# Probabilities of an attention loop transposed through memory instead of on TensorE, for all four units of a period

## The chip, the cores and the metric

One core of one Trainium2 chip runs the whole program. The metric is the device time of one execution in microseconds. Its engines are TensorE (PE, matrix products; PEld is its weight load), VectorE (DVE), ScalarE (ACT), GpSimd (POOL) and SyncE (SP, which here only issues transfers); 16 DMA engines carry the transfers of all queues.

## What is computed

A cross attention and then a routed feed-forward layer, each added to its input. The attention has 16 sequences (b), 256 queries and 256 keys each, 16 heads of 64:

```python
q = (x @ w_q).reshape(B, Sq, HEADS, DIM_HEAD).transpose(0, 2, 1, 3)
k = (context @ w_k).reshape(B, Skv, HEADS, DIM_HEAD).transpose(0, 2, 1, 3)
v = (context @ w_v).reshape(B, Skv, HEADS, DIM_HEAD).transpose(0, 2, 1, 3)
sim = jnp.einsum('bhid,bhjd->bhij', q, k) * SCALE
attn = jax.nn.softmax(sim, axis=-1)
out = jnp.einsum('bhij,bhjd->bhid', attn, v)
...
x = x + _L0_xattn_ref(_layernorm(x, axis=-1), ctx_768, ...)
x = x + _L0_ffn_ref(_layernorm(x, axis=-1), ...)
```

The feed-forward layer scores each of 4096 rows for 8 experts, takes the best two, sends rows to experts with room for 640 each, and sums the two experts' outputs by their gates. All numbers are float32; products that need it are made of three terms, a high part and a rest of each operand (`qh`, `ql` and so on).

## The kernel before

**Periods.** The attention loop has 64 periods, m = 0 to 63, four to a sequence: b = m // 4, r = m % 4. A period has four units, one head each. Its stages are `scores` (L801, into PSUM banks 0 to 3), row maxima `max0` to `max3` on DVE (L1255), exponentials `exp0` to `exp3` on ACT (L1067, into `prob`), and two periods later `pv` (L839), which multiplies transposed probabilities `probt` with `v`. In between the probabilities are transposed. `q`, `k` and `v` are the projections for the next period (L734); their halves are written by ACT (`q_hi`, `k_hi`) and DVE (`q_lo`, `k_lo`). The result of `pv` is multiplied by the inverse sums in place in PSUM (`a_norm`, L1274), and split into `ah` (ACT, `a_hi`) and `al` (DVE, `a_lo`). `o` (L855) is the output projection, twice a sequence, `xt` and `x2t` are transposes of a sequence's rows, `logits` and `pos` belong to the routing, as do `bias`, `shift`, `compare`, `rank`, `gate`, `slot`, `keys` and `pick` on DVE and `scatter` on POOL (L668), which writes rows into the experts' table in memory.

**Two ways to transpose.** In the moved periods (`MOVED`, 6 to 61) units 0 and 1 go through memory: DVE transposes 32x32 squares in place (`square0`, `square1`, L1279), SP writes the half to memory (`lift`, L485) and, once it has landed, reads it back with four transfers that put the squares in their places (`move`, L492). Units 2 and 3 are transposed on PE (`turn2`, `turn3`, L819, four transposes against the identity each) and copied out of PSUM by ACT (`copy2`, `copy3`, L1007). In the other periods all four units are turned on PE.

**Inverse sums.** DVE takes them (`inv`), SP writes them out (`inv_out`, L466) and reads them back spread over partitions (`inv_in`, L475), into one buffer `invrows`; so `inv_in` of period m - 1 waits for the `a_norm` of period m - 2.

**Order.** `timeline()` writes down one list of stages; each engine runs its own stages of that list in that order. Waits are on semaphores. Products other than scores and turns share three PSUM banks in turn (`WORKS`, `bank`); each waits until the user of its bank three before has been read. `logits` and the turns use bank 4.

**After the loop** come the expert products, in the stretch from about 700 us on, which nothing here touches.

## Time and profile before

| | us |
|---|---|
| median of three runs | 956.02 |
| lowest and highest | 954.73, 957.37 |
| the profiled execution | 957.82 |
| its span, first to last instruction | 956.1 |

| engine | busy us | share |
|---|---|---|
| PE | 918.1 | 96% |
| DVE | 739.8 | 77% |
| ACT | 573.8 | 60% |
| POOL | 280.2 | 29% |

The page of the profile gives such shares for the whole span. Views of a stretch give them for that stretch; the chain of waits gives, from start to start, what each piece took on the way to the end. A line such as L819 is a line of the kernel above; L734, L1007 and L1201 are helpers that several stages share.

### The profile page before, as it was taken

How to read it: one execution, taken by the hardware profiler on the slowest of the kernel's cores; microseconds unless marked ns; L12 is line 12 of the kernel's file. 1: busy time of each engine (PE TensorE's matmuls, PEld its weight loads, DVE VectorE, ACT ScalarE, POOL GpSimd, SP SyncE). 2: the span in 40 equal slices, each digit the busy share in tenths (PEclk: the TensorE clock that was granted, in tenths of full speed). 3: DMA queues.
4: the chain of work that ended last, by engine and by line, in shares of the span. 5: the costliest groups of instructions: out<-in, count | busy, mean ns of one | idle time of the engine just before them, and what ended most of it. 6: DMA issues, size and time to landing. Idle time of an engine off the chain costs nothing.

```text
span 956.1 us, 22462 instructions
## 1 busy us (share of the span) xinstructions
PE 918.1 (96%) x7916; PEld 821.0 (86%) x7916; DVE 739.8 (77%) x1745; ACT 573.8 (60%) x1600; POOL 280.2 (29%) x441
## 2 busy tenths in 40 slices
PE   7999999999999999999999999999889999999995
PEld 7878888888888888888888888888689999999995
DVE  5757778888888888888888888877777877678762
ACT  5877766667667666766766677676534433334420
POOL 5541112314233231323223132302533223322233
PEclk9999999999999999999999999999899999999999
DMA  8462535445455445455444445444345765645422
GB/s 239 143 205 91 163 123 163 162 152 168 146 157 158 148 157 164 136 172 164 139 156 161 146 130 170 136 134 136 121 133 99 149 145 123 135 84 98 112 29 27
DMA packets 152991, 133.29 MB, mean 139 GB/s; under 512 B 62140, under 2 KB 141610, under 8 KB 152752
## 3 DMA queue, kind: packets, MB, share of 16 engines
q1 hardware_dynamic: 144048, 122.87, 42.9%
q0 software_dynamic: 8832, 8.98, 5.4%
q8 instruction: 64, 1.05, 0.5%
q14 instruction: 47, 0.39, 0.1%
HBM read 82.15 MB, written 54.61 MB: 143 GB/s over the span
## 4 chain that ended last, share of the span: by engine, by line
PE 70%; DVE 11%; ACT 10%; issue 4%; DMA 3%; POOL 0%; SPq 0%; POOLq 0%; ACTq 0%; DVEq 0%
PE psum L734 20%; PE psum L839 9%; PE psum L996 9%; PE psum L855 9%; PE psum L980 8%; PE psum L801 7%; ACT prob L1067 6%; PE psum L819 5%; DVE negmax L1255 3%; DVE hidl L1201 2%; DVE bufl L1201 1%; ACT probt L1007 1%; DVE hidh L1488 1%; PE psum L879 1%; DVE psum L1274 1%
## 5 line engine op out<-in xcount | busy, mean ns | idle before, releaser
L1067 ACT ACTIVATE prob<-psum,negmax 128x256 f32<-128x256 f32 x512 | 238.0, 481 | 79.5 <-DVE negmax L1255 79.4
L1255 DVE TENSOR_REDUCE negmax<-psum 128x2 f32<-128x512 f32 x256 | 160.4, 682 | 29.7 <-PE psum L801 29.7
L1173 ACT ACTIVATE hid<-psum,b1t 128x640 f32<-128x640 f32 x64 | 50.9, 795 | 126.6 <-PE psum L980 125.0
L839 PE MATMUL psum<-probt,v 128*64 128x256 f32 x1024 | 124.6, 385 | 0.0
L707 POOL DMA_INDIRECT out_rows<-y,rowi x40 | 66.3, 1658 | 160.8 <-DVE y L1498 154.2
L1067 ACT ACTIVATION_READ_ACCUMULATOR prob<-psum,negmax 128x1 f32 x512 | 109.5, 214 | 0.0
L839 PEld LDWEIGHTS psum<-probt,v 128*64 128x64 f32 x1024 | 67.8, 136 | 36.4 <-issue 0.3
L668 POOL DMA_INDIRECT slot_table<-row,picki x64 | 66.8, 1044 | 96.9 <-PE psum L734 61.2
L996 PE MATMUL psum<-w2h,hidh 128*128 128x256 f32 x320 | 91.4, 286 | 2.9 <-DVE y L1498 1.5
L801 PE MATMUL psum<-kh,qh 64*128 64x256 f32 x512 | 82.5, 316 | 11.1 <-ACT prob L1067 8.9
L996 PE MATMUL psum<-w2l,hidh 128*128 128x256 f32 x320 | 90.5, 283 | 0.0
L996 PE MATMUL psum<-w2h,hidl 128*128 128x256 f32 x320 | 90.5, 283 | 0.0
L1007 ACT ACTIVATE probt<-psum 128x512 f32<-128x512 f32 x144 | 87.3, 609 | 4.4 <-PE psum L819 4.4
L819 PE MATMUL psum<-ident,prob 128*128 128x128 f32 x576 | 87.1, 276 | 2.7 <-ACT prob L1067 2.7
L734 PE MATMUL psum<-xth,wqh 128*128 128x256 f32 x256 | 78.9, 308 | 0.5 <-DVE xtl L1201 0.5
L1279 DVE STREAM_TRANSPOSE prob<-prob 128x512 f32<-128x512 f32 x112 | 78.6, 702 | 0.0
L855 PE MATMUL psum<-woh,ah 128*128 128x256 f32 x256 | 72.9, 285 | 1.6 <-DVE al L1201 1.6
L606 POOL TENSOR_SCALAR shifted<-ln_mean_var 128x2 f32<-128x2 f32 x32 | 7.1, 223 | 225.0 <-issue 182.7
L801 PE MATMUL psum<-kl,qh 64*128 64x256 f32 x512 | 72.9, 278 | 0.0
L801 PEld LDWEIGHTS psum<-kh,qh 64*128 64x128 f32 x512 | 48.8, 185 | 27.9 <-ACT prob L1067 13.3
L801 PE MATMUL psum<-kh,ql 64*128 64x256 f32 x512 | 72.8, 277 | 0.0
L855 PE MATMUL psum<-wol,ah 128*128 128x256 f32 x256 | 72.4, 283 | 0.0
(199 smaller groups left out, 2704.6 us busy)
## 6 DMA issues: line engine op xcount, KB each, us to landing
squares<-prob SPq DMA_DIRECT2D x56, 512.0 KB
probt<-squares SPq DMA_DIRECT2D x224, 128.0 KB, 2.8
invrows<-inverses SPq DMA_DIRECT2D x128, 128.0 KB
w1r<-in_w SPq DMA_DIRECT2D x8, 1024.0 KB
w2r<-in_w SPq DMA_DIRECT2D x8, 1024.0 KB, 9.1
slot_table<-blank SPq DMA_DIRECT2D x8, 662.5 KB, 6.5
blocks<-slot_table SPq DMA_DIRECT2D x56, 80.0 KB
xin<-in_x SPq DMA_DIRECT2D x16, 256.0 KB, 3.5
```

Source lines behind the costliest of these rows:

```text
L668: pool.indirect_dma_start(out=table, out_offset=bass.IndirectOffsetOnAxis(ap=picki[:, b % 3, k, t:t + 1], axis=0), in_=row[:, b % 3, t, :] ...
L734: mm = pe.matmul(dst, lhs, rhs, start=(j == 0), stop=(j == len(terms) - 1))
L801: mm = pe.matmul(psum[:, 2 * cc + h, qb * S:(qb + 1) * S], a[r, m % 2, cc, cols], w[r, m % 2, cc, :], start=(j == 0), stop=(j == len(terms ...
L819: mm = pe.transpose(psum[:, TURN_BANK[u], kb * S + qb * P:kb * S + (qb + 1) * P], prob[:, m % 2, u, kb, qb, :], ident[:, :])
L839: mm = pe.matmul(dst[h * HD:(h + 1) * HD, cc * S:(cc + 1) * S], v[:, b % 2, kb, cols], p, start=(kb == 0), stop=(kb == ST - 1))
L855: mm = pe.matmul(dst[:, 0:D], a[:, b % 2, c, tt], w[:, c, :], start=(c == 0 and j == 0), stop=(c == PAIRS - 1 and j == 2))
L980: mm = pe.matmul(dst, lhs, rhs, start=(n == 0), stop=(n == len(terms) - 1))
L996: mm = pe.matmul(dst, a[:, j, ss], w[:, j, :], start=(j == 0 and m == 0), stop=(j == HC - 1 and m == 2))
L1007: copy = lambda dst, src, **kw: act.activation(dst, src, ACT.Copy, **kw)
L1067: last = act.activation(into, out_of, ACT.Exp, bias=negmax[:, m % 2, u, qb:qb + 1], accum_out=total[:, m % 2, u, qb:qb + 1])
L1255: dve.tensor_reduce(negmax[:, m % 2, u, :], psum[:, u, :].rearrange("p (q s) -> p q s", q=ST), AX.X, ALU.max, negate=True).then_inc(sem("m ...
L1279: dve.transpose(at, at).then_inc(sem("square"), 1)
```

## The change

All four units of a moved period go through memory. `by_pe` is empty there, so PE has no `turn2` and `turn3` and ACT no copies. DVE transposes two units in one instruction, twice a period. `lift` writes 1 MB instead of 512 KB, and the four reads take 256 KB each in rows of 2 KB; SP issues two of them (`move_low`) and ACT the other two, behind its last exponential of the next period (`move_high`). An exponential now waits for the lift of two periods before, not for the moves.

`invrows` has two buffers, so `inv_in` waits for the `a_norm` of a period earlier, and `a_norm` stands behind `k_lo`. It writes to a new buffer `attended` in SBUF instead of PSUM, and the bank is free once it is done. A fourth work bank comes in with bank 4, and `logits` takes a work bank. Three pieces of DVE work go to POOL: `a_lo` (periods 4 to 59), `ln1` of later sequences, and the second half of `pick` (DVE keeps its two reductions as `extremes`). `x2t` moves from r = 2 to r = 3, `logits` and `bias` to r = 0, where `shift`, `compare`, `rank` and `gate` stand in both. The context has one load buffer instead of two. The core of the diff:

```diff
+POOL_REST = range(PER_B, PERIODS - 4)
...
-    return (2, 3) if m in MOVED else (0, 1, 2, 3)
+    return () if m in MOVED else (0, 1, 2, 3)
...
-        out += [("scores", m)] + ([("pv", m - 2)] if m >= 2 else [])
-        out += [("logits", b - 2)] if r == 3 and 2 <= b else []
...
         else:
-            out += [("q", m + 1), ("turn2", m - 1), ("k", m + 1), ("turn3", m - 1), ("v", m)]
+            out += [("scores", m)] + ([("logits", b - 3)] if r == 0 and 3 <= b else [])
+            out += [("q", m + 1), ("k", m + 1), ("pv", m - 2), ("v", m)]
...
         else:
-            out += [("copy2", m - 1), ("k_hi", m + 1), ("exp2", m), ("copy3", m - 1), ("exp3", m), ("v_sb", m)]
+            out += [*steps("exp0 exp1", m), ("q_hi", m + 1), ("exp2", m), ("k_hi", m + 1), ("exp3", m),
+                    ("move_high", m - 1), ("a_hi", m - 2), ("v_sb", m)]
...
-        out += ([("a_norm", m - 2)] if m >= 2 else []) + [("inv", m - 1)]
...
-        out += ([("a_lo", m - 2)] if m >= 2 else []) + [("q_lo", m + 1)]
-        out += [("square0", m)] if m in MOVED else []
-        out += [("k_lo", m + 1)]
...
+        else:
+            out += [("inv", m - 1)] + ([("slot", b - 3)] if r == 2 and 3 <= b else [])
+            out += [("x2add", ST * (b - 2) + 1)] if r == 1 and 2 <= b else []
+            out += [("bias", b - 3)] if r == 0 and 3 <= b else []
+            out += [("q_lo", m + 1), ("square0", m), ("k_lo", m + 1), ("a_norm", m - 2)]
...
-            out += [("ln1", b + 1)] if 1 <= b < B - 1 else []
...
-        out += [("pick", b - 3)] if r == 3 and 3 <= b else []
...
+        out += [("ln1", b + 1)] if r == 0 and 1 <= b < B - 1 else []
         out += [("scatter", b - 4)] if r == 0 and 4 <= b else []
         out += [("residual", b + 1)] if r == 0 and 1 <= b < B - 1 else []
+        out += [("a_lo", m - 2)] if m - 2 in POOL_REST else []
...
-        out += steps("inv_out inv_in", m - 1) + (steps("lift move", m) if m in MOVED else [])
+        out += [("extremes", b - 3), ("pick", b - 3)] if r == 3 and 3 <= b else []
...
+        out += [("inv_out", m - 1)] + ([("move_low", m - 1)] if m - 1 in MOVED else [])
+        out += [("traffic", b - 2)] if r == 1 and 2 <= b else []
+        out += [("inv_in", m - 1)] + ([("lift", m)] if m in MOVED else [])
...
-WORK_READ = {"xt": "xt_lo", "q": "q_lo", "k": "k_lo", "v": "v_sb", "pv": "a_lo", "o": "x2", "x2t": "x2t_sb",
+WORK_READ = {"xt": "xt_lo", "q": "q_lo", "k": "k_lo", "v": "v_sb", "pv": "a_norm", "o": "x2", "x2t": "x2t_sb",
...
+def places():
...
+    banks, last, found = [5, 6, 7], {}, {}
+    for stage, n in TIMELINE:
+        work = stage.removesuffix("_most"), n
+        if (stage, n) == ("turn0", PERIODS - 2):
+            banks.remove(4)
+            found[stage, n] = 4, last[4]
+        if work in WORKS and work not in found:
+            at = banks.pop(0)
+            banks.append(at)
+            found[work] = at, last.get(at)
+            last[at] = work
+        if (stage, n) == ("turn3", MOVED[0] - 1):
+            banks.append(4)
+    return found
+
...
-        invrows = sb(rest, "invrows", [2, S])
+        invrows = sb(rest, "invrows", [2, 2, S])
...
+        def move(eng, m, groups):
+
+            eng.wait_ge(sem("lifted"), 16 * (m - MOVED[0] + 1))
+            eng.wait_ge(sem("pv"), m - 1)
+            for g in groups:
+                eng.dma_start(probt_all(m)[g * SQ:(g + 1) * SQ, :].rearrange("j (a c) -> j a c", a=GROUPS),
+                              square_table[m % 2].rearrange("(a j) (g c) -> g j a c", a=GROUPS, g=GROUPS)[g])\
+                   .then_inc(sem(f"moved{m % 2}"), 16)
+
...
-                if m >= 1:
-                    sp.wait_ge(sem("a_norm"), m)
+                if m >= 2:
+                    sp.wait_ge(sem("a_norm"), m - 1)
                 for h in range(2):
-                    sp.dma_start(invrows[h * HD:(h + 1) * HD, :, :],
+                    sp.dma_start(invrows[h * HD:(h + 1) * HD, m % 2, :, :],
                                  inv_table[m % 2][0:UNITS * ST].rearrange("(c h q) p -> h c (q p)", h=2, q=ST)[h]
                                  .partition_broadcast(HD))\
...
-                sp.dma_start(square_table[m % 2], prob_pair(m)).then_inc(sem("lifted"), 16)
...
+                sp.dma_start(square_table[m % 2], prob_all(m)).then_inc(sem("lifted"), 16)
...
+            def ln1(b):
+                pool.wait_ge(sem("xt"), b)
+                if b >= XRING:
+                    pool.wait_ge(sem("logits"), b - XRING + 1)
+                for t in range(ST):
+                    last = pool.tensor_scalar(xn[:, t, :], xin[:, b % XRING, t, :], mean_var["ln1"][:, t, 0:1],
+                                              rstd["ln1"][:, t:t + 1], ALU.subtract, ALU.mult)
+                last.then_inc(sem("ln1"), 1)
...
+            def a_lo(m):
+                b, c = divmod(2 * m, PAIRS)
+                pool.wait_ge(sem("a_hi"), m + 1)
...
+                pool.tensor_tensor(al[:, b % 2, c:c + 2, :], attended[:, :, :],
+                                   ah[:, b % 2, c:c + 2, :].bitcast(F32), ALU.subtract).then_inc(sem("a_lo"), 1)
+
+            def pick_(b):
+                pool.wait_ge(sem("extremes"), b + 1)
+                if b >= 3:
+                    pool.wait_ge(sem(f"scatter{b % 3}"), 16 * 2 * ST * (b // 3))
+                pool.tensor_scalar(pick[:, 0, :], pick[:, 0, :], BIG, None, ALU.add)
+                link(pool.tensor_scalar(pick[:, 1, :], pick[:, 1, :], -1.0, None, ALU.add))
+
+                link(pool.tensor_tensor(same[:, 0, :], pick[:, 1, :], pick[:, 0, :], ALU.subtract))
+                link(pool.tensor_scalar(same[:, 0, :], same[:, 0, :], 0.0, BIG, ALU.is_le, ALU.mult))
+                link(pool.tensor_tensor(pick[:, 1, :], pick[:, 1, :], same[:, 0, :], ALU.add))
+                pool.tensor_copy(picki[:, b % 3, :, :], pick[:, :, :]).then_inc(sem("picks"), 1)
...
-                    pool.wait_ge(sem("q"), PER_B * (b + 4) + 2)
+                    pool.wait_ge(sem("k"), PER_B * (b + 4) + 2)
...
-                            if m in MOVED and cc == 0:
-                                p = probt_pair(m).rearrange("p (a u k q i) -> p u k q a i", a=GROUPS, u=2, k=ST, q=ST)[:, h, kb]
+                            if m in MOVED:
+                                p = probt_all(m).rearrange("p (a u k q i) -> p u k q a i", a=GROUPS, u=UNITS, k=ST,
+                                                           q=ST)[:, 2 * cc + h, kb]
                             else:
                                 p = probt[:, m % 2, 2 * cc + h, kb, :]
...
+                if m >= 2 and m - 2 not in MOVED:
                     act.wait_ge(sem("turn"), turns_to(m - 2, u))
                 elif m >= 2:
-                    act.wait_ge(sem(f"moved{m % 2}"), 16 * moves_to(m - 2))
+                    act.wait_ge(sem("lifted"), 16 * (m - 2 - MOVED[0] + 1))
                 for qb in range(ST):
...
-                dve.wait_ge(sem("inv_in"), 32 * (m + 1))
-                at = work_bank("pv", m).rearrange("p (c s) -> p c s", c=2)
-                dve.tensor_tensor(at, at, invrows[:, :, :], ALU.mult).then_inc(sem("a_norm"), 1)
-
-            def square(m, u):
-                dve.wait_ge(sem("exp"), UNITS * m + u + 1)
-                at = prob_pair(m).rearrange("p (g u c) -> p u g c", g=GROUPS, u=2)[:, u]
+                dve.wait_ge(sem(f"inv_in{m % 2}"), 32 * (m // 2 + 1))
+                if m >= 1:
+                    dve.wait_ge(sem("a_lo"), m)
+                dve.tensor_tensor(attended[:, :, :], work_bank("pv", m).rearrange("p (c s) -> p c s", c=2),
+                                  invrows[:, m % 2, :, :], ALU.mult).then_inc(sem("a_norm"), 1)
+
+            def square(m, pair):
+
+                dve.wait_ge(sem("exp"), UNITS * m + 2 * pair + 2)
+                at = prob_all(m).rearrange("p (g v c) -> p v g c", g=GROUPS, v=2)[:, pair]
                 dve.transpose(at, at).then_inc(sem("square"), 1)
...
+            def extremes(b):
+                dve.wait_ge(sem("keys"), b + 1)
+                if b >= 1:
+                    dve.wait_ge(sem("picks"), b)
+                dve.tensor_reduce(pick[:, 0, :], lowkey[:, :, :], AX.X, ALU.min)
+                dve.tensor_reduce(pick[:, 1, :], high_of(b), AX.X, ALU.max).then_inc(sem("extremes"), 1)
```

The order of the instructions shows it at three places. On PE, in a moved period, `q` is followed by the turn of a unit and then `k` before:

```order
L734 MATMUL psum<-xth,wql 128x256
L819 MATMUL psum<-ident,prob 128x128 [waits s_exp]
L819 MATMUL psum<-ident,prob 128x128 x3
L734 MATMUL psum<-c0h,wkh 128x256 [waits s_ctx,s_v_sb]
L734 MATMUL psum<-c0l,wkh 128x256
L734 MATMUL psum<-c0h,wkl 128x256
```

and after, where `k` ends and `pv` and `v` follow:

```order
L797 MATMUL psum<-c1s,wkh 128x256
L797 MATMUL psum<-c1s,wkl 128x256
L904 MATMUL psum<-probt,v 64x256 [waits s_probt,s_moved1,s_v_sb]
L904 MATMUL psum<-probt,v 64x256 x7
L797 MATMUL psum<-wvh,c0h 128x512 [waits s_ctx,s_x2]
```

No turn stands there, and `pv` has moved from ahead of `q` to behind `k`. On DVE, in a period with r = 3 (`negmax` are the maxima, `invrows` the inverse sums, `prob` the squares, `pick` and `picki` the routing's slots), before:

```order
L1255 TENSOR_REDUCE negmax<-psum 128x2 [waits s_scores] x4
L1274 TENSOR_TENSOR psum<-psum,invrows 128x512 [waits s_inv_in,s_pv]
L1264 RECIPROCAL invtot<-total 128x8 [waits s_inv_out,s_exp]
L1267 STREAM_TRANSPOSE invturned<-invtot 128x32 [waits s_inv_total]
L1334 TENSOR_TENSOR logit<-psum,rb_all 128x16 [waits s_logits]
L1201 TENSOR_TENSOR al<-psum,ah 128x512 [waits s_a_hi]
L1244 SCALAR_TENSOR_TENSOR ql<-psum,qh 128x512 [waits s_q_hi]
L1279 STREAM_TRANSPOSE prob<-prob 128x4x128 [waits s_exp]
L1201 TENSOR_TENSOR kl<-psum,kh 128x512 [waits s_k_hi]
L1279 STREAM_TRANSPOSE prob<-prob 128x4x128 [waits s_exp]
L1431 TENSOR_REDUCE pick<-lowkey 128x2 [waits s_scatter1,s_keys]
L1432 TENSOR_REDUCE pick<-highkey 128x2
```

and after:

```order
L1325 TENSOR_REDUCE negmax<-psum 128x2 [waits s_scores] x4
L1334 RECIPROCAL invtot<-total 128x8 [waits s_inv_out,s_exp]
L1337 STREAM_TRANSPOSE invturned<-invtot 128x32 [waits s_inv_total]
L1314 SCALAR_TENSOR_TENSOR ql<-psum,qh 128x512 [waits s_q_hi]
L1352 STREAM_TRANSPOSE prob<-prob 128x4x256 [waits s_exp]
L1271 TENSOR_TENSOR kl<-psum,kh 128x512 [waits s_k_hi]
L1345 TENSOR_TENSOR attended<-psum,invrows 128x512 [waits s_a_lo,s_inv_in1,s_pv]
L1352 STREAM_TRANSPOSE prob<-prob 128x4x256 [waits s_exp]
L1502 TENSOR_REDUCE pick<-lowkey 128x2 [waits s_picks,s_keys]
L1503 TENSOR_REDUCE pick<-highkey 128x2
```

`al` is gone, the squares are twice as long, and the multiplication by `invrows` stands behind `kl` and waits for POOL's `a_lo` of the period before. On ACT the end of a period with r = 0 is after:

```order
L1072 ACTIVATE kh<-psum 128x512 [waits s_scores,s_k]
L1133 ACTIVATE prob,total<-psum,negmax 128x2x4x32 [waits s_lifted,s_max]
L1133 ACTIVATE prob,total<-psum,negmax 128x2x4x32
L433 DMA probt<-squares 32x4x512 [waits s_pv,s_lifted]
L433 DMA probt<-squares 32x4x512
L1072 ACTIVATE ah<-attended 128x512 [waits s_o,s_a_norm]
L1072 ACTIVATE v<-psum 128x512 [waits s_pv,s_v]
L1191 ACTIVATE lexp<-lshift 128x16 [waits s_shifted]
```

The two copies into `probt` are gone, two transfers stand behind the last exponential, and `ah` has moved behind them. On POOL a period with r = 0 now holds the context, `ln1`, the four scatters, the residual and then `a_lo`; before it held the context, the scatters and the residual. Its scatters wait for `k` now and waited for `q`.

## Rows read from the trace of the kernel before

**Rows 1.** The page, busy us (share of the span) and instructions of each engine.

```profile
PE 918.1 (96%) x7916; PEld 821.0 (86%) x7916; DVE 739.8 (77%) x1745; ACT 573.8 (60%) x1600; POOL 280.2 (29%) x441
```

**Rows 2.** Busy time by stretch, one sequence; last: granted clock, DMA share, GB/s.

```profile
390.57:432.61 42.04, 41.30 (x380) 35.58 (x379) 35.34 (x93) 29.11 (x92) 11.68 (x23) 1.00 0.49 157
```

**Rows 3.** The chain of waits, 417 to 442: start us, us, engine, tile, line.

```profile
420.57 0.42 PE psum L879 x16
...
430.10 1.64 PE psum L734 x12
431.74 0.44 PE psum L819 x4
432.18 1.19 PE psum L734 x10
...
433.80 1.16 PE psum L734 x5
434.96 2.86 PE psum L855 x24
437.82 1.62 PE psum L801 x24
439.44 1.88 PE psum L839 x16
```

**Rows 4.** PE's timeline: start, duration, instruction, [idle before, who ended it].

```profile
410.71 0.39 PE L734 MATMUL psum<-c0h,wkh 128*128 128x256 f32 x1 [0.26 <-DVE valid L1382]
...
427.25 0.39 PE L801 MATMUL psum<-kh,qh 64*128 64x256 f32 x2 [0.49 <-ACT prob L1067]
```

**Rows 5.** The chain of waits again, a `pv` ahead of the moved periods.

```profile
71.20 1.88 PE psum L839 x16
```

**Rows 6.** DVE's transposes, whole span: count, busy us, mean ns of one.

```profile
L1279 DVE STREAM_TRANSPOSE prob<-prob 128x512 f32<-128x512 f32 x112 | 78.6, 702 | 0.0
...
L1470 DVE STREAM_TRANSPOSE turned<-blocks 128x640 f32<-128x640 f32 x14 | 11.6, 834 | 0.0
```

**Rows 7.** DVE's timeline in a period with r = 3.

```profile
424.92 0.69 DVE L1201 TENSOR_TENSOR kl<-psum,kh 128x512 fp32r<-128x512 f32 x1 [0.33 <-ACT kh L1007]
425.53 0.70 DVE L1279 STREAM_TRANSPOSE prob<-prob 128x512 f32<-128x512 f32 x1
...
426.39 0.17 DVE L1433 TENSOR_SCALAR pick<-pick 128x2 f32<-128x2 f32 x1
...
427.30 2.47 DVE L1255 TENSOR_REDUCE negmax<-psum 128x2 f32<-128x512 f32 x4
```

**Rows 8.** Busy time by stretch of 1 us, during a lift and during moves.

```profile
407.00:408.00 1.00, 1.00 (x13) 0.64 (x10) 1.00 (x3) 0.20 (x1) 0.54 (x3) 1.00 0.90 359
411.00:412.00 1.00, 1.00 (x10) 1.00 (x10) 1.00 (x2) 0.78 (x2) 0.00 (x0) 1.00 0.82 266
```

**Rows 9.** SP's waits (total us, times, longest), and its timeline: one period's moves.

```profile
SPq L492 <- DMA squares<-prob: 174.1, 56, 4.8
...
421.35 1.75 SPq L492 DMA_DIRECT2D probt<-squares  x4
```

**Rows 10.** POOL in one sequence, and in its timeline behind the scatters.

```profile
L631 POOL TENSOR_TENSOR xin<-xin,bo_all 128x256 f32<-128x256 f32 x2 | 1.5, 727 | 2.2 <-DMA slot_table<-row,picki 2.1
...
440.59 1.54 POOL L631 TENSOR_TENSOR xin<-xin,bo_all 128x256 f32<-128x256 f32 x2 [2.95 <-DMA slot_table<-row,picki]
```

**Rows 11.** DVE's groups in one sequence: idle before them, who ended it.

```profile
L1255 DVE TENSOR_REDUCE negmax<-psum 128x2 f32<-128x512 f32 x16 | 10.0, 681 | 1.2 <-PE psum L801 1.2
...
L1244 DVE SCALAR_TENSOR_TENSOR ql<-psum,qh 128x512 fp32r<-128x512 f32 x5 | 3.4, 690 | 1.1 <-ACT qh L1007 1.0
...
L1201 DVE TENSOR_TENSOR kl<-psum,kh 128x512 fp32r<-128x512 f32 x4 | 2.8, 692 | 1.0 <-ACT kh L1007 0.6 <-issue 0.3
...
L1201 DVE TENSOR_TENSOR xtl<-psum,xth 128x512 fp32r<-128x512 f32 x1 | 0.7, 691 | 1.1 <-ACT xth L1007 1.1
```

**Rows 12.** Busy time by stretch, the opening.

```profile
0.00:24.00 24.00, 18.70 (x148) 17.04 (x149) 13.86 (x23) 13.62 (x34) 12.73 (x26) 1.00 0.86 239
```

More of the change, by code:

```diff
@@ L214 @@
 TIMELINE = timeline()
-WORK_BANKS = 3
 TURN_BANK = (4, 0, 1, 4)
-APART = {**{("logits", b): 4 for b in range(B - 3)}, ("x2t", B - 2): 2, ("logits", B - 2): 3, ("pos", B - 2): 4, ("logits", B - 1): 4}
+APART = {("x2t", B - 2): 2, ("logits", B - 2): 3, ("pos", B - 2): 4, ("logits", B - 1): 4}
 GATHER = ((2, 3), (0, 1))
@@ L685, in _ @@
                     inverse_root(stage[:3], n)
+                if stage == "ln1" and n >= 2:
+                    ln1(n)
+                if stage == "a_lo" and n in POOL_REST:
+                    a_lo(n)
+                if stage == "pick" and n < B - 4:
+                    pick_(n)
                 if stage == "vsplit":
@@ L714, in _ @@
         def _(pe):
-            work = {w: n for n, w in enumerate(WORKS)}
             def bank(stage, n):
-                if stage == "logits" and n < B - 3:
-                    pe.wait_ge(sem("probt"), turns_to(PER_B * (n + 2) + 1, UNITS - 1))
-                    return psum[:, APART[stage, n], :]
                 if (stage, n) in APART:
@@ L1453, in _ @@
             for stage, n in TIMELINE:
-                if stage in steps:
+                if stage in steps and not (stage == "ln1" and n >= 2 or stage == "a_lo" and n in POOL_REST
+                                               or stage == "pick" and n < B - 4):
                     steps[stage](n)
```

139 lines of the change are left out of this document (72 added, 67 removed).

## The prediction, made before the changed kernel was run

> **What bounds the kernel now.** I read the page's busy shares first [rows 1]: TensorE (PE) is busy 918.1 of 956.1 us, VectorE (DVE) 739.8, ScalarE (ACT) 573.8, GpSimd (POOL) 280.2. PE is the bound, but an average does not say where the changed part stands, so the second view cuts the attention loop into rounds. A round is one sequence, four periods. A round takes 42.04 us (three in a row differ by 0.01), and in it PE is busy 41.3, DVE 35.35, ACT 29.1 and POOL 11.7 us at granted clock 1.00; the DMA engines have a share of 0.49 at 157 GB/s [rows 2]. Third comes the chain of waits, since its pieces show what each stage costs PE from start to start, without the overlap that the busy numbers count [rows 3]: scores 1.62, pv 1.88, q 1.64, k 1.19, v 1.16, o 2.86, logits 0.42, and each turn, four transposes, 0.44 us. xt and x2t are four transposes as well; pos, five tiny products, I put at 0.2.
>
> The round adds up. Without turns it is 4 x (1.62 + 1.88 + 1.64 + 1.19 + 1.16) = 29.96, plus 2 x 2.86, plus 0.44 + 0.44 + 0.42 + 0.2: **37.2 us of PE work**. The eight turns are 8 x 0.44 = 3.5. The remaining 42.04 - 37.2 - 3.5 = 1.3 us are gaps, and two of them can be seen: k waits 0.26 us for `valid`, that is for a bank, and scores wait 0.49 us for an exponential [rows 4].
>
> **The change, part by part.** *Turns removed.* In the 56 moved periods (14 rounds) PE loses turn2 and turn3: 112 x 0.44 = 49.3 us. PE does nothing in their place. The moved operand is read by pv in runs of 32 elements, for two units before and four after; that costs nothing, since pv took 1.88 us at 71.20, before any period was moved, and takes 1.88 us in the moved rounds [rows 3, 5]. ACT, busy 29.1 of 42 us, loses eight copies a round and gains eight DMA issues, about as much again; it stays far from a bound.
>
> *Double squares on DVE.* 128x512 takes 702 ns and 128x640 834 ns [rows 6]: 1.03 ns an element, so 128x1024 should take 1.23 us, 0.53 more than now. That is 8 x 0.53 = +4.2 us a round. Taken off DVE: four `al`, which step like `kl` by 0.61 us (424.92 to 425.53; -2.4), ln1's two applications (half an `al` each, -0.6), and five of the seven picking instructions (426.39 to 427.30, -0.9) [rows 7]. Net +0.3: DVE has some **35.7 us of work a round against PE's 37.2**. This is what makes the change close.
>
> *The order inside a period.* I lay a period out from the start of its scores, with the pieces above. PE: q done at 3.3, k at 4.5, pv at 6.3, v at 7.5. DVE: maxima from 0.95 to 3.4, inverse to 3.8, q_lo from 4.15, square0 to 5.9, k_lo to 6.5, a_norm (behind pv) to 7.1, square1 to 8.25, then the period's extras. ACT: exp3 ends near 6.3. Periods are 10.8 (r=0), 8.1 (r=1), 10.4 (r=2) and 7.9 us (r=3) of PE work; DVE's extras are 2.6, 2.0, 3.0 and 0.2 us. So DVE begins the maxima up to 0.9 us late behind r=1 and 0.7 late behind r=2, and is level again in r=3, whose extras are the smallest. The next scores need exp3 and k_lo, which are ready at 6.3 to 7.4 us even then, ahead of the shortest period's end at 7.9. PE does not wait on this path, with 0.5 to 3 us to spare. Both visible gaps should go: the exponentials no longer stand behind copies, and the fourth work bank gives `valid` a turn more.
>
> *Transfers.* Each lift is 1 MB and each period moves 1 MB. A round now carries 157 GB/s x 42 us = 6.6 MB [rows 2]; with 2.1 MB more each way it carries 10.8 MB. Engine time: 0.49 x 42.04 = 20.6 us now. A stretch with little but a lift ran at 359 GB/s with a share of 0.90, 401 at a full share; one with moves and other small packets at 266 GB/s with 0.82, 324 at a full share [rows 8]. The moves' packets double to 2 KB, so they lie between. Adding 2.1 MB at 401 and 2.1 MB at 324 to 401 gives 31.0 to 32.3 us in a round of 38: **a DMA share of 0.83**, against 0.49. In time: lifts land 3.1 us behind their issue now (174.1 us for 56) [rows 9]; doubled, about 4.5 to 5. Moves go out once the lift has landed, from SP near 5 us into the next period and from ACT behind exp3 at 6.3 to 7.2 (four issues take 1.75 us now [rows 9]), and land near 11. The pv that reads them starts at 12.5 in the short periods: 1 to 1.5 us to spare, least in r=1, where SP's x, output and context transfers (0.77 MB) run between the two halves.
>
> That the second half is issued from ACT saves SP's issue time only, as far as rows show: one pool of 16 engines carries all queues, and its share is what I sum. The Trainium skill, "DMA: Bandwidth & Descriptors", section "Issuing engines are not separate DMA queues", says the same in general: DMAs started from several engines run on the same 16 DMA engines and interleave, and only the sequencer's issue time is saved. By that rule the second queue brings no bandwidth, which speaks against this part of the change and for the DMA rivals below; by a rule of its own bandwidth for each queue those rivals would have no chance and the forecast would be the same.
>
> *Double inverse rows.* inv_in no longer waits for the a_norm of the same period, so a_norm can stand behind k. Same bytes, cost nothing; the cover is a whole period.
>
> *POOL* gains a_lo, ln1 and the rest of picking. 128x256 takes 727 ns [rows 10], so a_lo takes at most 1.45 us and I take 1.3, a fixed part being paid once; four of them, two ln1 and six small ones add 8 us to 11.7 us. The tight place is r=0: context, ln1, the scatters behind k (4.9 to 10.0), their landing (2.95 us now [rows 10]), residual 1.5, then a_lo done near 15.8. The next a_norm waits for it and could start at 17.1: 1.3 us to spare. If that is lost, DVE stands still with square1 behind it.
>
> *Before and after the moved rounds* the work is the same. At the end SP reaches the expert weights behind two moves instead of four: nothing to 1.5 us gained, I take nothing.
>
> **The sum.** PE's work of 37.2 us is the floor of a round, 42.04 the ceiling of "nothing gained". Of the 1.3 us of gaps I keep 0.9, as room for new waits where DVE and the transfers have about 1 us to spare: a round of 38.1 us. Saved: 3.94 x 14 = 55 us. The profiled execution is 957.8 us, 1.8 over the median 956.0: 957.8 - 55 = 902.6, and 901 against the median.
>
> **Rivals.**
> 1. *All gaps go*: 37.2 us a round, 4.84 x 14 = 68 saved: 888. For it: the laid-out period has no PE wait. Against it: DVE at 96% and DMA at 0.83 of their time.
> 2. *DVE becomes the bound.* If DVE keeps the waits that it has for q_hi, k_hi, xt_hi and the scores (1.0 + 0.6 + 1.1 + 1.2 = 3.9 us [rows 11]), its round is 35.7 + 3.9 = 39.6: 34 saved, 922. For it: they are waits for ACT's results, which the new order also has. Against it: several arise only because PE was behind.
> 3. *Moves land late.* The margin of 1 to 1.5 us in r=1 and r=3 goes, and pv waits 1 us in two periods: a round of 40.1, 27 saved, 929.
> 4. *DMA engines saturate* (slower). The only long stretch with a share near 1 is the opening, 239 GB/s at 0.86 [rows 12]. If squares, moves, broadcasts and scatters together reach only 239 GB/s, a round of 10.8 MB takes 45.2 us: +3.1 x 14 = 44 us, 1000. It decides from 257 GB/s (10.8 MB in 42.04 us) down.
> 5. *The turns go, but their time is idled*, by a chain of lift, move and pv that keeps today's period: 956.
>
> **How the numbers follow.** Forecast 0.50 (37.7 to 39.0 us a round: 895 to 914), rival 1 0.14, rivals 2 and 3 0.23 together, rival 4 0.07, rival 5 0.03, and 0.03 for a round between 40.1 and 42. The range leaves out rivals 4 and 5 and the last, and goes 3 us below rival 1 for the floor's own error: 885 to 935. A measurement of this kernel tells 0.3% (about 3 us) from no change; faster 0.89, same 0.04, slower 0.07.
>
> **What would show it.** Right: a round of about 38 us, PE busy over 95% of it (no transposes of `prob` on PE from the seventh period to the sixty-second), DVE's `prob` transposes near 1.23 us, a DMA share near 0.83. Rival 2 shows as PE idle before scores or before q, k, v, released by DVE, with DVE above 95% busy; rival 3 as PE idle before pv, released by `probt<-squares`; rival 4 as the same with shares near 1 and landings far over 5 us; a late a_lo as DVE idle before `attended`, released by POOL. The forecast is wrong if a round takes over 39.5 us, most likely because margins of 1 us, each laid out from one trace, do not hold together.

## The result and the profile after

The changed kernel takes **985.93 us** (median of 4 runs, 984.21 to 987.17) against 955.75 us (954.73 to 957.37) for the kernel before on the same chip: a ratio of 1.031, 95% interval 1.029 to 1.034. It is slower by 30 us where 55 us were forecast to be saved. The forecast of 901 us, its range (885 to 935) and its sign were wrong.

The page first, as [rows 1]: busy us and shares of each engine.

```profile
PE 891.5 (90%) x7468; PEld 794.0 (81%) x7468; DVE 744.6 (76%) x1601; ACT 510.7 (52%) x1488; POOL 400.8 (41%) x597
```

PE lost 448 instructions, the transposes, and its share fell from 96 to 90%: no engine has become the bound. Next the stretches, one of the loop in the kernel before and one in the changed kernel (columns as in [rows 2]).

```profile
252.00:294.00 42.00, 41.25 (x379) 35.58 (x377) 35.42 (x93) 29.08 (x93) 11.68 (x23) 1.00 0.48 153
```

```profile
252.00:294.00 42.00, 37.43 (x329) 31.79 (x328) 33.11 (x79) 23.76 (x80) 20.27 (x35) 0.96 0.84 252
```

In 42 us PE now does 329 matmuls, where 379 were done with the turns among them. DVE, ACT and POOL are all below 80%, and the DMA share has risen to 0.84. The granted clock is 0.96, between the 2.4 GHz level, at which it stood before, and 1.2 GHz; PE kept stopping in this stretch. The residual addition on POOL, once a round, opens at 238.72, 283.14, 327.66, 372.74 and 416.94 us, and five rounds on at 638.43: **a round takes 44.4 us** on average over these nine, against 42.04 before. The expert part behind the loop did not change (240 us from its first `hid` activation to the end, 241 before). What holds the round is told by the share of the chain of waits (page, part 4, by engine) and the waits for DMA (out, in, total us, times, longest).

```profile
DMA 33%; PE 23%; DVE 15%; SPq 8%; POOL 8%; issue 6%; ACT 6%; POOLq 0%; ACTq 0%; DVEq 0%
```

```profile
SPq L433 <- DMA squares<-prob: 204.9, 55, 6.6
...
POOL xin L692 <- DMA slot_table<-row,picki: 71.5, 11, 7.1
ACT ah L1072 <- DMA squares<-prob: 60.9, 20, 5.0
...
PE psum L904 <- DMA probt<-squares: 39.6, 37, 3.0
```

SP waits 3.7 us for nearly every lift, where it was 3.1 by [rows 9]; and there the wait began with the lift's issue, while now SP first issues `inv_out` and waits for its input, so 3.7 us is only the rest of the landing. ACT waits for lifts too, PE waits for moves, and POOL waits up to 7.1 us for the scatters (2.95 in [rows 10], 3.6 at most before). The landing times (page, part 6: count, size, median us from issue to landing) show how far the transfers have slowed each other.

```profile
squares<-prob SPq DMA_DIRECT2D x56, 1024.0 KB, 7.7
probt<-squares SPq DMA_DIRECT2D x112, 256.0 KB, 4.9
probt<-squares ACTq DMA_DIRECT2D x112, 256.0 KB, 5.8
invrows<-inverses SPq DMA_DIRECT2D x128, 128.0 KB, 6.0
```

The last view is the chain of waits through one round (start us, us, what). In this round it never touches PE.

```profile
352.92 8.97 DMA squares<-prob
361.91 0.31 SPq L433
...
362.27 0.43 SPq L433
...
362.80 0.60 SPq L510
...
363.45 0.60 SPq L510
...
364.15 9.45 DMA squares<-prob
373.62 0.31 SPq L433
...
378.96 6.95 DMA squares<-prob
...
388.62 6.53 DMA squares<-prob
...
397.38 8.95 DMA squares<-prob
```

A lift is issued 2.2 us (once 2.7) after the one before it landed. In between, SP issues two moves (L433) and two reads of inverse rows (L510); once a round (373.62 to 378.96) x, output and context are issued as well, 5.3 us. The four lifts of this round take 8.97 + 9.45 + 6.95 + 6.53 = 31.9 us; the other 12.6 of the 44.5 us from 352.92 to 397.38 are issues. **The loop through SP's queue is closed**: a lift's landing releases the moves of its period (1 MB, on two queues) and the inverse rows (256 KB), and then the next lift, which runs beside them. So the 1 MB lift has 1.25 MB beside it, issued shortly before, and 2304 KB in 7.7 us are 306 GB/s.

This is not the chain of every round. From 90 to 165 and from 307 to 430 us it is made of lifts and SP's issues almost alone; from 210 to 290 us it holds no lift, and 18 to 20% of it is the landing of the scatters, with POOL's and DVE's work behind it. Two chains of nearly the same length run through this kernel, and both have a transfer in them that became slower.

### The profile page after: what moved, and what is told of

Same layout as the page of the kernel before. It is cut to its first block, busy times and chain, and to the rows that moved or that the text cites. A ratio compares the mean times of both kernels' runs of the same rounds, so it can differ in the third digit from the quotient of the medians.

```text
span 985.4 us, 21333 instructions
## 1 busy us (share of the span) xinstructions
PE 891.5 (90%) x7468; PEld 794.0 (81%) x7468; DVE 744.6 (76%) x1601; ACT 510.7 (52%) x1488; POOL 400.8 (41%) x597
## 3 DMA queue, kind: packets, MB, share of 16 engines
q10 hardware_dynamic: 16128, 29.37, 10.0%
## 4 chain that ended last, share of the span: by engine, by line
DMA 33%; PE 23%; DVE 15%; SPq 8%; POOL 8%; issue 6%; ACT 6%; POOLq 0%; ACTq 0%; DVEq 0%
DMA squares<-prob 26%; PE psum L1061 9%; PE psum L1045 8%; DMA slot_table<-row,picki 5%; SPq L510 4%; ACT prob L1133 3%; DVE prob L1352 3%; SPq L433 2%; POOL slot_table L729 2%; PE psum L797 2%; POOL al L659 2%; DVE hidl L1271 2%; PE psum L904 1%; DVE bufl L1271 1%; DVE attended L1345 1%
## 5 line engine op out<-in xcount | busy, mean ns | idle before, releaser
L904 PE MATMUL psum<-probt,v 128*64 128x256 f32 x1024 | 129.0, 394 | 39.6 <-DMA probt<-squares 39.6
L659 POOL TENSOR_TENSOR al<-attended,ah 128x512 fp32r<-128x512 f32 x56 | 72.4, 1293 | 227.2 <-ACT ah L1072 226.3
L1352 DVE STREAM_TRANSPOSE prob<-prob 128x1024 f32<-128x1024 f32 x112 | 138.0, 1232 | 0.7 <-ACT prob L1133 0.7
L904 PEld LDWEIGHTS psum<-probt,v 128*64 128x64 f32 x1024 | 77.4, 140 | 72.3 <-issue 47.5
L1072 ACT ACTIVATE ah<-attended 128x512 fp32r<-128x512 f32 x64 | 40.5, 632 | 179.9 <-DVE attended L1345 97.5
L1133 ACT ACTIVATION_READ_ACCUMULATOR prob<-psum,negmax 128x1 f32 x512 | 114.1, 223 | 0.0
L1345 DVE TENSOR_TENSOR attended<-psum,invrows 128x512 f32<-128x512 f32 x64 | 43.8, 684 | 75.1 <-POOL al L659 55.0
L797 PE MATMUL psum<-xth,wql 128*128 128x256 f32 x256 | 75.1, 293 | 0.0
L797 PE MATMUL psum<-xtl,wqh 128*128 128x256 f32 x256 | 74.9, 293 | 0.0
L797 PEld LDWEIGHTS psum<-xth,wqh 128*128 128x128 f32 x256 | 50.8, 198 | 29.3 <-DVE attended L1345 21.9
```

Of the source, the lines that this page charges most:

```text
L659: pool.tensor_tensor(al[:, b % 2, c:c + 2, :], attended[:, :, :], ah[:, b % 2, c:c + 2, :].bitcast(F32), ALU.subtract).then_inc(sem("a_lo" ...
L797: mm = pe.matmul(dst, lhs, rhs, start=(j == 0), stop=(j == len(terms) - 1))
L904: mm = pe.matmul(dst[h * HD:(h + 1) * HD, cc * S:(cc + 1) * S], v[:, b % 2, kb, cols], p, start=(kb == 0), stop=(kb == ST - 1))
L1133: last = act.activation(into, out_of, ACT.Exp, bias=negmax[:, m % 2, u, qb:qb + 1], accum_out=total[:, m % 2, u, qb:qb + 1])
L1352: dve.transpose(at, at).then_inc(sem("square"), 1)
```

## The experiments

Four theories. **A**: transfers, either by their number of bytes or by this loop. **B**: POOL's chain; in r = 1 `attended` stood still for `al`, and `al` was behind the residual, which waited for scatters:

```profile
375.79 0.69 DVE L1345 TENSOR_TENSOR attended<-psum,invrows 128x512 f32<-128x512 f32 x1 [5.55 <-POOL al L659]
```

```profile
372.74 1.55 POOL L692 TENSOR_TENSOR xin<-xin,bo_all 128x256 f32<-128x256 f32 x2 [6.83 <-DMA slot_table<-row,picki]
374.37 1.29 POOL L659 TENSOR_TENSOR al<-attended,ah 128x512 fp32r<-128x512 f32 x1
```

**C**: ACT, which now stands in front of its moves for the lift (60.9 us above). **D**: the new order itself. All edits are on the changed kernel, timed in three rounds beside the kernel before. The code shows the core of each edit; `...` stands for more of the same kind.

**half_bytes.** The lift carries the first 1024 of 2048 columns, each move 256 of 512.

```
-  sp.dma_start(square_table[m % 2], prob_all(m))
+  sp.dma_start(square_table[m % 2][:, 0:1024], prob_all(m)[:, 0:1024])
...
```

> The changed kernel with every lift cut to 512 KB and every move to 128 KB, as they were before; all instructions, their order and all other transfers stay (so half of what pv reads is old: this kernel leaves out half of the transposed probabilities). Theory A, transfers: a lift lands 7.7 us behind its issue because the moves of the period before and the inverse rows run beside it, and SP, which issues the next lift only behind that landing, closes the loop. Then a lift lands in 3.5 to 4.5 us, a round falls from 44.5 to 38 or 39 us, and the time to 895 to 915 us. Theory B, POOL: residual waits for the scatters, al behind it, and DVE's attended for al, 5 us a round. The scatters would still have the same place: 950 to 985. Theory C, ACT stands still at its move behind the lift: as A, since the lift lands earlier. Theory D, DVE's longer squares and the new order themselves: 975 to 986.

Measured 915.46 us, ratio 0.956 (0.953 to 0.957). A round takes 39.6 us, at the upper edge of what A foretold. Of the theories, A is right: 70 of the 85 us between forecast and result hang on 59 MB. D can't be the cause, since the longer squares and the new order are all still there.

**short_loop, residual_first, one_queue.** Three changes of order, bytes untouched. In short_loop SP issues inverse rows and traffic ahead of the moves, so that the next lift follows the moves at once; in residual_first POOL's residual comes ahead of the scatters; in one_queue all four moves are SP's.

```
-  out += [("inv_out", m - 1)] + ([("move_low", m - 1)] if m - 1 in MOVED else [])
+  out += steps("inv_out inv_in", m - 1)
   out += [("traffic", b - 2)] if r == 1 and 2 <= b else []
-  out += [("inv_in", m - 1)] + ([("lift", m)] if m in MOVED else [])
+  out += [("move_low", m - 1)] if m - 1 in MOVED else []
+  out += [("lift", m)] if m in MOVED else []
```

> The changed kernel with SP's order in a period as inv_out, inv_in, traffic, move_low, lift, so that between one lift's landing and the next lift's issue SP has only two issues (0.8 us) instead of 2.2 us and in every fourth period 5.2. Theory A, if the loop through SP is what binds: about 4 x 1.3 + 3 = 8 us less a round, down to the next bound of 38 to 40 us: 905 to 930. Theory A, if the rate of the DMA engines binds (share 0.83 now, all transfers still meet): the landing grows by what the loop loses, 965 to 985. Theories B, C and D: no change, 980 to 990.

> The changed kernel with POOL's residual ahead of the scatters instead of behind them, so that al of that period no longer waits for the scatters to land. Theory B: DVE's wait for al (55.0 us in 11 times) goes, 930 to 950. Theory A: the loop through SP sets the round; the chain of waits runs through it and not through POOL, so 975 to 986. C and D: as A.

> The changed kernel with all four moves issued by SP and none by ACT. Theory C: ACT's 61 to 70 us at the lift's landing go, and what follows from them: 930 to 960. Theory A, loop: two more issues of 0.43 us between landing and next lift, 56 periods, 0.9 us each: 1020 to 1035; theory A, rate: 980 to 1000. B and D: no change.

Measured: short_loop 1047.67 us (ratio 1.094, 1.092 to 1.096), residual_first 989.79 (1.034, 1.031 to 1.036), one_queue 1021.09 (1.066, 1.064 to 1.068). residual_first took `al` out of DVE's waits (55.0 us before the edit, none of note after it) and gained nothing, so B alone is not the bound. From 100 to 600 us its chain of waits now runs over the lifts throughout, 50 to 82% of each 100 us: with the one chain gone, the other sets the same time. one_queue took lifts off ACT's path and lost 35 us; the two issues of some 0.4 us that it adds to the loop in each of 56 periods are worth that and more (48 us), so C falls. short_loop was a miss of its expectation, and its waits say why (SP's own; then PE's):

```profile
SPq L511 <- DMA inverses<-invturned: 184.0, 62, 7.3
```

```profile
PE psum L905 <- DMA probt<-squares: 89.8, 39, 6.0
```

`inv_in` waits for a small write (`inverses`, 16 KB) that now has to pass the same 16 engines as the big ones; SP waited up to 7.3 us for it (2.5 at most before). Put ahead of the moves, this wait holds them back. In the changed kernel SP waited for this write only 8 times, 18.8 us in all, since the moves stood in between.

**act_moves2, split_lift.** Two attempts to open the loop with the bytes kept. In act_moves2 ACT issues all four moves, so that no lift stands behind one; in split_lift the lift is two halves in 1 KB rows, each issued when its square is done.

```
+  for half in range(2):
+      if half:
+          sp.wait_ge(sem("square"), 2 * (m - MOVED[0] + 1))
+      sp.dma_start(square_table[m % 2].rearrange("p (g v c) -> v p g c", g=GROUPS, v=2)[half],
+                   prob_all(m).rearrange("p (g v c) -> p v g c", g=GROUPS, v=2)[:, half])
...
```

> The bytes of the changed kernel, but all four moves are issued by ScalarE and none by SyncE, so that a lift on SyncE no longer stands behind the landing of the lift before it. If the loop through SyncE's queue sets the time: 940 to 965 us. If the rate of the DMA engines sets it: 980 to 990 us. If ScalarE's wait for the lift is what costs, it now stands before four issues instead of two: over 990 us.

> The bytes of the changed kernel, but the lift is two transfers of 512 KB in rows of 1 KB, each issued as soon as its own half of the probabilities is turned (about 4 us between them). If the closed loop from turn to landing to the next lift sets the time, the first half lands before the second starts and the loop shrinks by 2 to 3 us in a period: 945 to 970 us. If the rate of the 16 DMA engines sets it, the bytes are as many: 980 to 990 us.

Measured 1027.33 us (1.073, 1.071 to 1.075) and 999.13 us (1.044, 1.042 to 1.046). Both missed what the loop through SP alone foretells. In act_moves2 SP no longer waits for a lift, but the lifts' median landing rises to 8.8 us and the moves' to 6.1, and PE stands 93.9 us for them (39.6 in the changed kernel). It may be that a lift that leaves earlier meets more of the moves before it. But the edit also closes another loop: all moves now stand behind ACT's exponentials. In its chain of waits the last exponentials of a period end at 324.77 us, ACT issues the moves to 326.33, a move lands 9.88 us later, and `pv` follows. The expectation had this as its third case (over 990 us), and the two were not told apart. split_lift did not open the loop: lifts and SP's issues fill its chain of waits from 300 to 600 us. It has eight times the packets in its lifts (1 KB instead of 8 KB each) and one more issue in the loop; those two were not told apart either. So neither run says whether the queue alone is the cause; the runs with fewer bytes do.

**half_lift, half_moves.** Which half of the added bytes costs? In half_lift the lift carries 512 KB and the moves are whole; in half_moves it is the other way about.

> The lift of a period carries 512 KB instead of 1 MB; the four moves keep their size (each reads one half again, so the probabilities are wrong there). Half of the added bytes go. If the loss is the number of bytes: halfway between half_bytes and the changed kernel, 945 to 955 us. If the loop from turn to lift landing to the next lift sets the time, more than half is won, since the 7.7 us landing is what shrinks: 920 to 935 us.

> The lift is whole (1 MB), and each of the four moves carries 128 KB instead of 256 KB (half of the transposed probabilities is left out). If the loss is the number of bytes: 945 to 955 us, as half_lift. If the loop through the lift's landing sets the time, less is won, since only what runs beside the lift shrinks: 955 to 970 us.

Measured 967.67 us (1.010, 1.008 to 1.013) and **913.99 us** (0.955, 0.953 to 0.957). Both expectations missed. With half the moves the whole loss is gone, though each lift still carries 1 MB. The 18 lifts on its chain of waits took 4.0 to 6.6 us (6.5 to 9.8 in the changed kernel), with half the moves beside them; two of them:

```profile
314.18 4.93 DMA squares<-prob
...
355.60 4.09 DMA squares<-prob
```

and the loop is open most of the time (lifts are 10% of the chain over the span, 26% in the changed kernel). Of SP's waits, in the changed kernel the first row was the lift's; in half_moves:

```profile
SPq L501 <- DVE invturned L1337: 255.9, 63, 9.4
...
SPq L433 <- DMA squares<-prob: 41.0, 28, 3.0
...
SPq L520 <- DVE prob L1352: 24.6, 31, 2.8
```

SP waits mostly for DVE's inverse sums (L1337) and squares (L1352) of the next period, as it should, and 41.0 us for lifts where it was 204.9. In half_lift the lifts, half as large, still landed in 7.2 us beside whole moves. But half_lift had a fault of its own, seen in the queues (page, part 3; packets, MB, share), first of the changed kernel and then of half_lift; q10 carries ACT's moves alone:

```profile
q10 hardware_dynamic: 16128, 29.37, 10.0%
```

```profile
q10 hardware_dynamic: 16128, 29.37, 13.8%
```

0.100 x 16 x 985.4 us over 16128 packets is 98 ns each, 0.138 x 16 x 966.6 is 132. In half_lift moves of two queues read the same bytes at the same time.

**half_lift_b, thin_rows.** half_lift with each move reading its own part; and the changed kernel with the inverse rows cut to 32 of 256 columns.

```
+  few = slice(0, 1024 if m > MOVED[0] + 1 else 2048)
+  sp.dma_start(square_table[m % 2][:, few], prob_all(m)[:, few])
```

> half_lift mended: there two moves on two queues read the same half of the table, and a packet of ScalarE's moves took 132 ns against 98 ns in the changed kernel. Here the lift carries 512 KB from the third middle period on, and each move reads its own part of the table, partly stale. If that double reading was what set half_lift (967.7 us) apart from half_moves (914.0 us): 915 to 925 us. If full moves are what the program can't take, whoever lifts: 955 to 970 us.

> The changed kernel, with the two inverse-row reads of each middle period cut to 32 of 256 columns (32 KB in place of 256 KB; the other rows are stale there). They are issued between the moves and the next lift and run beside both. If the time is that of the bytes in flight (2.25 MB in 7.7 us, so 0.75 us for 224 KB), each of 56 periods gets shorter by that: 986 - 42 = 944, so 935 to 955 us. If the small packets of these reads cost nothing beside the large ones: 980 to 986 us.

Measured 939.12 us (0.980, 0.977 to 0.982) and 954.79 us (0.995, 0.991 to 0.999). half_lift_b lies between its two expectations. Reading the same bytes twice had cost half_lift 29 us; a packet of ACT's moves now takes 107 ns. thin_rows gains 31 us for 224 KB a period, 0.55 us of every period where 0.75 was expected. By bytes alone (70 us for 59 MB) these 12.6 MB would have been worth 15. The round follows what is in flight together: with 2304, 2080 and 1792 KB (changed kernel, thin_rows, half_lift_b) it takes 44.4, 42.6 and 41.2 us. But half_moves, also 1792 KB, takes 39.3, so the number of bytes is not all. That whole moves cost more than whole lifts is shown; in half_lift_b they land in 4.7 to 5.7 us and PE still stands 11.7 us before `pv`, in half_moves in 2.9 to 3.1 and it doesn't. The queues say where the time goes (as above; half_moves, then half_lift_b):

```profile
q1 hardware_dynamic: 127920, 137.55, 47.4%
q10 hardware_dynamic: 16128, 14.69, 5.6%
```

```profile
q1 hardware_dynamic: 127920, 123.92, 48.9%
q10 hardware_dynamic: 16128, 29.37, 11.5%
```

With almost the same bytes the two queues hold all 16 engines for 0.530 x 911.4 = 483 us in half_moves and for 0.604 x 937.6 = 566 us in half_lift_b. The changed kernel stands at 0.632 x 985.4 = 623: the second half of the moves takes 140 us of all engines, 210 GB/s, the second half of the lifts 57 us, about 500. What makes a move's bytes the dearer ones (2 KB packets, reading from memory, 32 rows of the target) was not isolated.

**mix_all, mix_all_b, mix_two, mix_two_b.** The control for D: the new order, but two units moved and two turned, in all middle periods (mix_all) or in those with r = 0 and 1 (mix_two). The turns use banks 1 and 0. In the first pair `pv` stood behind both turns; the second pair has it ahead of the first (the lines below, against the first pair).

```
-  out += [("q", m + 1)] + ([("turn2", m - 1)] if two else []) + [("k", m + 1)]
-  out += ([("turn3", m - 1)] if two else []) + [("pv", m - 2), ("v", m)]
+  out += [("q", m + 1)] + ([("pv", m - 2), ("turn2", m - 1)] if two else []) + [("k", m + 1)]
+  out += ([("turn3", m - 1)] if two else [("pv", m - 2)]) + [("v", m)]
```

> The order of the changed kernel is kept, but each middle period moves only two units of probabilities through memory, as before, and TensorE turns the other two again (into banks 1 and 0): the bytes and the turns of the kernel before in the new order. If the added bytes are the whole cause, the time is that of half_bytes (915.5 us) plus 112 turns of 0.44 us, 945 to 965 us. If the new order, the remainders on GpSimd or the double inverse rows cost something of themselves, it is over 970 us.

> As mix_all, but only the periods r = 0 and r = 1 of a round move two units; r = 2 and r = 3 move all four. The added bytes are halved and taken out of the periods that also carry residual rows and scatters. If the loss is the meeting of transfers: 915.5 us plus 56 turns of 0.44 us = 940 us where the moves land in time, so 930 to 955 us, below the kernel before. If each full lift costs its 8 us whatever its neighbours do, half of the 70 us stays: 970 to 980 us.

> mix_all with the same step moved, so that it is again the control for the new order with the bytes and the turns of the kernel before. TensorE stood 44 us before its turns in mix_all (1003.5 us). If these waits were the whole of it: 955 to 965 us, and the order by itself costs nothing. If the order costs by itself: 980 us or more.

> mix_two with one step moved: in the periods with turns TensorE does the product pv ahead of the first turn instead of behind the second. In mix_two TensorE stood 39.3 us before those turns, for the exponentials of the second unit, and never for a move. If that wait was what held mix_two (978.9 us), most of it goes: 940 to 950 us, under the kernel before. If the lift's landing or VectorE held it, the wait turns up elsewhere: 965 to 980 us.

Measured: mix_all 1003.45 us (1.048, 1.047 to 1.050), mix_two 978.88 (1.022, 1.019 to 1.026), mix_all_b **962.38** (1.006, 1.004 to 1.007), mix_two_b 965.58 (1.011, 1.007 to 1.014). mix_all was a poor control, and its PE group says so: `turn2` needs bank 1 free, and only `q` lay between scores and it.

```profile
L895 PE MATMUL psum<-ident,prob 128*128 128x128 f32 x576 | 89.1, 278 | 46.5 <-ACT prob L1147 44.0 <-ACT probt L1084 1.7 <-issue 0.6
```

With `pv` in that place 41 us are back: one step in the wrong place costs three quarters of the 55 us that the change was to bring. mix_all_b shows that the new order with the old bytes and turns costs 0.4 to 0.7%, so D explains 4 to 7 us. mix_two_b, with the bytes halved in two of four periods, missed its 940 to 950. SP waits for its lifts 78.6 us, far less than in the changed kernel, but POOL still waits 46.2 us for the scatters, and from 100 to 600 us their landing is the largest transfer on its chain of waits (10%); in which periods it loses was not looked at.

**three.** The middle amount in every period: three units through memory (768 KB each way), and one turned into bank 0 behind `k`, where its exponentials have long been done.

```
-    return () if m in MOVED else (0, 1, 2, 3)
+    return (0, 1, 2, 3) if m not in MOVED else (3,)
...
-            out += [("q", m + 1), ("k", m + 1), ("pv", m - 2), ("v", m)]
+            two = len(by_pe(m - 1)) == 1
+            out += [("q", m + 1), ("k", m + 1)] + ([("turn3", m - 1)] if two else []) + [("pv", m - 2), ("v", m)]
...
-                at = prob_all(m).rearrange("p (g v c) -> p v g c", g=GROUPS, v=2)[:, pair]
+                at = prob_all(m).rearrange("p (g c) -> p g c", g=GROUPS)[:, :, (0, 256)[pair]:(256, 384)[pair]]
```

> Three of the four units of a period move through memory (lift and moves of 768 KB each), and TensorE turns the fourth into bank 0, behind q and k, where its exponentials are long done. The bytes beside each other are those of half_moves (1.5 MB for lift and moves together, 914.0 us), the turns cost 56 times 0.44 us. If the loss is that full lifts and full moves of neighbouring periods don't fit beside each other: 914 + 25 = 939, so 930 to 945 us, below the kernel before. If the moves' own landing sets the time, as half_lift hints: about 950 to 960 us.

Measured **932.63 us** (931.8 to 934.88), ratio 0.972 (0.970 to 0.974): 2.8% under the kernel before and 5.4% under the changed one, with all outputs computed.

```profile
294.00:336.00 42.00, 41.54 (x376) 34.90 (x376) 34.47 (x83) 28.13 (x93) 21.56 (x37) 1.00 0.68 205
```

```profile
squares<-prob SPq DMA_DIRECT2D x56, 768.0 KB
probt<-squares SPq DMA_DIRECT2D x112, 192.0 KB, 4.5
probt<-squares ACTq DMA_DIRECT2D x112, 192.0 KB, 4.2
```

PE is busy 99% of this stretch and of its neighbours from 210 to 462 us, at granted clock 1.00, and the DMA share is 0.68 to 0.77. A round is 40.6 us, half_moves' 39.3 and 4 x 0.44 for the turns less 0.5.

## Why the prediction was wrong

- **The turns** went as said: no transposes of `prob` on PE in the moved periods, and where transfers don't interfere the kernel runs at 914 us, 42 below before, of the 49.3 priced.
- **DVE** was priced well. The 128x1024 transpose takes 1232 ns (forecast 1.23 us), and in half_bytes DVE is busy 149.19 us in 168, 35.2 in a round of 39.6 (forecast 35.7). `a_lo` on POOL takes 1293 ns (forecast 1.3).

```profile
L659 POOL TENSOR_TENSOR al<-attended,ah 128x512 fp32r<-128x512 f32 x56 | 72.4, 1293 | 227.2 <-ACT ah L1072 226.3
L1352 DVE STREAM_TRANSPOSE prob<-prob 128x1024 f32<-128x1024 f32 x112 | 138.0, 1232 | 0.7 <-ACT prob L1133 0.7
```

- **The floor of a round** was too low. In half_moves PE is busy 459.12 of the 470 us from 100 to 570, which is 38.4 us of a round of 39.3, against the 37.2 that the sum had as pure work. Half of the missing 1.2 us stood in [rows 2]: PE busy 41.3 of 42.04 leaves 0.7 us idle, where the sum called 1.3 us gaps. So forecast 38.1 was out of reach. That is 1.2 x 14 = 17 us, about the 13 us between 901 and 914. It is the smaller part.
- **The transfers' engine time** was priced by stretches at 324 to 401 GB/s at a full share [rows 8]. The queues say otherwise (page, part 3: packets, MB, share of 16 engines), q1 of the kernel before and then of the changed one, whose q10 is shown above:

```profile
q1 hardware_dynamic: 144048, 122.87, 42.9%
```

```profile
q1 hardware_dynamic: 127920, 152.23, 53.2%
```

(0.532 + 0.100) x 985.4 - 0.429 x 956.1 = 213 us of all 16 engines for 58.7 MB more: 276 GB/s if all of it is put down to them, or 15.2 us a round where 10.4 to 11.7 were summed. In a round of 38 us the share would have been (20.6 + 15.2) / 38 = 0.94, not 0.83. The mis-sized term is the moves': priced at 324 to 401 GB/s, their added half took 140 us, 210 GB/s, or 10.0 us a round where 5.2 to 6.5 were summed; the lifts' added half was priced at 401 and took 423 GB/s (from half_bytes, 0.452 x 915.2 = 414 us, to half_moves, 483). The short stretches of [rows 8] had one kind of transfer almost alone.
- **The landing of a lift** is the step that failed. 3.1 us for 512 KB, "doubled, about 4.5 to 5", took a lift that ran beside little and let it stay so. It landed in 7.7, because the change makes it run beside the moves and inverse rows of the period before it. Nothing in the prediction asked what is in flight when a lift is issued. In half_moves, with less beside them, lifts of the same size did take 4.0 to 6.6 us.
- **The loop through SP** was not in the prediction at all. Margins of 1 to 1.5 us at each `pv` were taken against the period that PE sets; with the landing at 7.7 us and 2.2 us of issues behind it, the loop itself sets the period (four times 9.9, and 3.1 for x, output and context: 42.7 us, above PE's work), and no margin at `pv` can give it back. The issues were known (1.75 us for four moves, [rows 9]) but counted for the moves only, not for the lift behind them.
- **The scatters** held POOL up to 7.1 us where 2.95 was taken from [rows 10]; the margin of 1.3 us at `a_norm` was lost, as warned. That made a second chain of the loop's length; residual_first shows that taking it away alone gains nothing. In half_moves the scatters' longest wait is 3.2 us again, with POOL's order as in the changed kernel: this too hung on the transfers.
- **The rivals.** Rival 4 had the right cause family, total transfers, and a price (1000 us) closest to the result, at a chance of 0.07. Its bound, 239 GB/s from the opening [rows 12], was what the loop came to (227 to 252 GB/s), at shares of 0.75 to 0.84. That these are not near 1 does not refute it, since the opening stood at 0.86. What speaks against one fixed rate is half_lift_b: it carries half_moves' bytes, at 202 to 217 GB/s in the loop, and a round still takes 41.2 us against 39.3. So it matters which bytes they are, not only how many. The chance was too low because the deciding point, 257 GB/s, lies above a rate that a row of this trace had already shown. Rival 3 had the place, `pv` waiting for moves, which is there (39.6 us) but follows from late lifts. Rival 2's round of 39.6 us is what half_bytes measures, yet in half_moves PE is busy 98% of a round of 39.3, so it was mostly the floor. DVE is close behind: it has 30% of half_bytes' chain of waits, 11% before.
- **The rule on queues** (the Trainium skill, "DMA: Bandwidth & Descriptors", section "Issuing engines are not separate DMA queues"), that transfers started from several engines interleave on the same 16 DMA engines: the trace agrees. Moves on ACT's queue shared the engines with SP's lifts (with half the moves, the lifts on the chain fell from 6.5 to 9.8 us to 4.0 to 6.6), and moving all moves to ACT did not make them land sooner (6.1 us; 4.9 and 5.8 before). What the second queue did bring was issue time outside the loop: one_queue, without it, is 35 us slower.

## What to carry to other kernels

Price a transfer by what will be in flight beside it, not by its landing in the old trace: follow the issuing queue round once (landing, the issues that the landing releases, the next issue) and compare that loop with the period that the engines set. When a tuned loop trades engine work for traffic, try the middle amount before the whole: here two units moved give 956 us (962 in the new order), three 933 and four 986. Taking away one of two chains of the same length gains nothing; look for what both have in common. And a control that changes an order must leave the cover of each waiting step as it was, or it measures its own wait.

## What was not expected of the hardware

Large transfers slow small ones two to three times: the write of the inverses had SP waiting 2.5 us at most before and 7.3 us in short_loop, and the read of 128 KB of inverse rows landed in 3.1 us in half_bytes and 6.0 in the changed kernel. Two queues that read the same bytes of memory at the same time cost a quarter more per packet than when each read its own (132 against 107 ns; 98 in the changed kernel). The added bytes of the moves, reads in 2 KB packets, held the engines twice as long as the added bytes of the lifts, writes in 8 KB packets (210 GB/s against 423). And the price of traffic has a knee: 29 MB less in the moves was worth 72 us, and another 29 MB less in the lifts (half_bytes) worth nothing, though without the cut in the moves it was worth 47 (half_lift_b).
